# Branch steps dealt out among 64 chunks of a dense layer on ACT and DVE: another table of places, three places in a chunk

## What is computed

```python
x = x + tanh(g_xattn[0]) * wkv(w, u, layernorm(x), ctx)
x = x + tanh(g_ffn[0]) * einsum('bsh,dh->bsd', fwht(silu(xn @ W1.T) * (xn @ W3.T)), W2)   # xn = layernorm(x)
x = x + tanh(g_xattn[1]) * wkv(-exp(time_decay), time_first, layernorm(x), ctx)
x = x + tanh(g_ffn[1]) * moe(layernorm(x))    # top 2 of 8, silu(h1) * h3, combined by gate weights
```

## Time and profile before

| | us |
|---|---|
| three runs | 1480.81, 1480.82, 1476.43 |
| median | 1480.81 |
| the profiled execution | 1483.66 |
| its span | 1482.0 |
| PE, DVE, ACT, POOL busy | 1244.8, 726.9, 504.1, 201.2 |
| the 64 chunks | 113.3 to 743.1 |

### The profile page before, as it was taken

The page is one execution under the profiler, slowest core; times in us unless marked ns, Lnnn a source line. Parts: engine busy times, 40 slices in busy tenths (PEclk is TensorE's granted clock), DMA queues, the critical chain, the costliest instruction groups (busy, mean ns, idle before and its releaser), DMA issues. The chain is left out here.

```text
span 1482.0 us, 18672 instructions
## 1 busy us (share of the span) xinstructions
PE 1244.8 (84%) x5785; PEld 590.9 (40%) x5786; DVE 726.9 (49%) x1175; ACT 504.1 (34%) x671; POOL 201.2 (14%) x206
## 2 busy tenths in 40 slices
...
GB/s 253 29 114 136 178 248 220 171 191 171 254 166 85 181 197 219 214 95 260 213 204 208 46 182 160 146 121 179 186 138 189 178 201 134 163 120 100 77 67 61
DMA packets 228347, 239.13 MB, mean 161 GB/s; under 512 B 137168, under 2 KB 141520, under 8 KB 225168
## 3 DMA queue, kind: packets, MB, share of 16 engines
...
## 5 line engine op out<-in xcount | busy, mean ns | idle before, releaser
L1084 PE MATMUL PS<-weights,xs 128*128 x1872 | 412.9, 381 | 29.5 <-DMA xs<-X 29.5
L1009 PE MATMUL PS<-xs,weights 128*128 128x512 f16 x1536 | 358.4, 390 | 26.8 <-DVE sg L845 15.1
L1084 PEld LDWEIGHTS PS<-weights,xs 128*128 128x128 f16 x1872 | 183.8, 98 | 252.3 <-issue 33.3
L1009 PEld LDWEIGHTS PS<-xs,weights 128*128 128x128 f16 x1536 | 152.6, 100 | 222.9 <-issue 24.2
L912 DVE SCALAR_TENSOR_TENSOR A<-A,PS 128x1024 f32<-128x1024 f32 x39 | 47.6, 1221 | 352.2 <-PE PS L1084 324.1
L1021 PE MATMUL PS<-weights,hs 128*128 128x512 f16 x768 | 181.3, 387 | 0.0
L604 ACT ACTIVATE A<-PS 128x1024 f32<-128x1024 f32 x39 | 39.9, 1024 | 320.1 <-PE PS L1084 192.2
L364 POOL DMA_INDIRECT row_list<-entry,pos x32 | 38.5, 1204 | 790.8 <-DVE pos L795 454.8
L923 DVE TENSOR_SCALAR V<-PS,outl 128x512 f32<-128x512 f32 x39 | 29.3, 751 | 166.7 <-PE PS L1098 150.6
L1021 PEld LDWEIGHTS PS<-weights,hs 128*128 128x128 f16 x768 | 76.4, 100 | 86.2 <-issue 6.6
L1098 PE MATMUL PS<-weights,xs 128*128 x456 | 104.0, 386 | 7.9 <-DMA weights<-e 4.6
...
## 6 DMA issues: line engine op xcount, KB each, us to landing
e<-halves SPq DMA_DIRECT2D x192, 256.0 KB
...
V<-ctx_cm ACTq DMA_DIRECT2D x7, 1024.0 KB, 5.7
X<-w ACTq DMA_DIRECT2D x4, 1024.0 KB, 6.1
out<-X ACTq DMA_DIRECT2D x4, 1024.0 KB, 9.9
...
```

What stands on the lines that cost most here:

```text
L1009: ins = te.matmul(bank(bk), wj[:, j, w, a, c * P:(c + 1) * P], xs[:, g % 2, b, c, :], start=(k == 0 and c == 0), stop=(k == 2 and c == C - 1))
L1084: ins = te.matmul(bank(n), xTt[k][:, b, c, :], weights_of(off, 2 * I // NT * c + n, a), start=(c == 0 and m == 0), stop=(c == C - 1 and m ...
```

## The change

It changes tables and places, no arithmetic.

- UNITS, STEPS, FIRST, GATES, GATE_STEPS and LATE have other numbers. Branches begin 9 or 10 chunks apart. The first branch in the chunks has its own, shorter tail (SHORT). Pieces 2 to 7 are split in chunks 1, 2, 3, 5, 6, 7.
- There are three places. On ACT: place 0 before the silu, place 1 between silu (and first unit) and high copy, place 2 at the chunk's end behind the units. On DVE: place 0 before the product, place 1 behind the low half, place 2 at the end. PE keeps its two.
- k0 takes its own half of the bonus on E1, k1 the other half; den is all scans of V, num has none.
- The turned rows of a post branch go into the place of the group's rows in X (`turned_rows`) and not into E1, except in the last. So xh0 of a post branch waits for the store of those rows (`x3_out`), e0 no longer waits for "last", and the unit buffers in X are lent when "last" of post 0 has run.

```diff
-UNITS = [[3, 3, 3, 3, 0, 3, 3, 3, 2, 3, 3, 3, 4, 4, 4, 2],
-         [3, 3, 3, 2, 4, 4, 4, 4, 2, 3, 4, 3, 2, 3, 3, 3],
...
+UNITS = [[3, 3, 3, 3, 0, 1, 2, 3, 2, 0, 4, 4, 4, 2, 4, 4],
+         [4, 4, 4, 0, 4, 4, 4, 2, 4, 4, 4, 3, 3, 0, 3, 3],
...
-STEPS = [("stats", 0, 0), ("r0", 0, 0), ("newton", 0, 0), ("norm", 1, 0), ("kT0", 1, 1), ("e0", 2, 0), ("k0", 2, 0),
...
+STEPS = [("stats", 0, 0), ("r0", 0, 2), ("newton", 1, 0), ("norm", 1, 1), ("kT0", 2, 0), ("e0", 2, 1), ("k0", 2, 2),
+         ("kT1", 3, 0), ("e1", 3, 1), ("k1", 3, 2), ("ln", 4, 1), ("den", 4, 2), ("rec", 4, 2), ("num", 5, 2), ("mix", 6, 2),
+         ("yT0", 7, 1), ("add0", 8, 0), ("yT1", 8, 1), ("add1", 9, 0), ("r2", 9, 1), ("newton2", 9, 2), ("norm2", 10, 1),
+         ("xT0", 11, 0), ("xh0", 11, 0), ("xl0", 11, 0), ("xT1", 11, 1), ("xh1", 12, 0), ("xl1", 12, 0), ("last", 12, 1),
+         ("raw", 12, 1)]
...
-FIRST = {("pre", 1): 0, ("pre", 2): 11, ("post", 0): 20, ("pre", 3): 30, ("post", 1): 39, ("post", 2): 49}
+FIRST = {("pre", 1): 0, ("pre", 2): 9, ("post", 0): 19, ("pre", 3): 29, ("post", 1): 39, ("post", 2): 49}
...
-GATES = {0: (31, 32, 34, 34, 35), 1: (50, 51, 53, 53, 54), 2: (60, 61, 62, 61, 62)}
+GATES = {0: (38, 41, 44, 44, 45), 1: (54, 58, 58, 59, 59), 2: (62, 63, 63, 63, 63)}
...
-LATE = {1: 2, 2: 3, 4: 4, 7: 5, 9: 6, 10: 7}
+LATE = {1: 2, 2: 3, 3: 4, 5: 5, 6: 6, 7: 7}
...
+        turned_rows = lambda g: E1[:, :] if g == NG - 1 else xg(g)
...
-                            sp.wait_ge(s["x3_out"], 16)
+                            sp.wait_ge(s["side_full"], FILLS.index(("post", 0, "last")) + 1)
...
-                        if posts_before(b):
-                            act.wait_ge(s["side_full"], FILLS.index(("post", posts_before(b) - 1, "last")) + 1)
...
-                        act.activation(ch(E1, a, 2), side, ACT.Copy).then_inc(s["kt_done"], 1)
+                        if g < NG - 1:
+                            act.wait_ge(s["x3_out"], 16 * (g + 1))
+                        act.activation(ch(turned_rows(g), a, 2), side, ACT.Copy).then_inc(s["kt_done"], 1)
...
+                    bonus(layer, E1, SQ, (0, 1))
                 elif step == "k1":
...
-                    bonus(layer, E1, SQ, (0, 1))
+                    bonus(layer, E1, SQ, (2, 3)).then_inc(s["den_done"], 1)
                 elif step == "den":
-                    bonus(layer, E1, SQ, (2, 3)).then_inc(s["den_done"], 1)
-                    scan(layer, A1, V, (0, 1, 2))
+                    scan(layer, A1, V, range(C))
                 elif step == "num":
-                    scan(layer, A1, V, (3,))
```

More of the change, by code:

```diff
@@ L95, in steps_beside @@
         if (kind, gb) in FIRST:
-            found += [(kind, gb, s) for s, d, at in STEPS if FIRST[kind, gb] + d == n and at == place]
+            steps = [(s,) + SHORT.get(s, (d, at)) if (kind, gb) == ("pre", 1) else (s, d, at) for s, d, at in STEPS]
+            found += [(kind, gb, s) for s, d, at in steps if FIRST[kind, gb] + d == n and at == place]
         if kind == "post" and gb in GATES:
@@ L553, in chunk @@
                     w_high(LATE[n])
-                for u in units[0:1]:
-                    unit_high(u)
                 if n >= 2:
```

28 lines of the change are left out of this document (17 added, 11 removed), and 7 rows, old and new, of tables (STEPS, UNITS).

## The result

| | before | after |
|---|---|---|
| median of four runs, us | 1478.62 | 1509.98 |
| lowest to highest | 1476.02 to 1480.82 | 1505.82 to 1513.53 |
| the profiled execution, its span | 1483.66, 1482.0 | 1508.1, 1506.4 |
| the 64 chunks | 113.3 to 743.1 | 111.3 to 773.7 |

The change makes the kernel slower: ratio 1.0212, 95% interval 1.0175 to 1.0249. The forecast was 1486 us with a range up to 1503; the sign was right and the size was not.

A forecast was written before the change was run, and what follows sets the result against it. The 64-chunk loop can't be under 539 us of PE work; 90.7 us were lost. New losses 36.8 + 31.9 + 23.7 + 1.1 + 0.5 + 2.0 = 96.0, 5.3 more: 1486 us, own range 1478 to 1494, with rivals 1456 to 1503.

The forecast's parts named there:

- The waits of kT0 and yT0: PE waits 27.3 us at kT0 opening five chunks, 36.8 with clock; DVE's late mixed rows hold yT0, 4.3 in chunk 26.
- The residual sum in 33: On DVE, the residual sum now behind k1 holds chunk 32's down matmuls by 2.4 us.
- The cost of chunk 63: gate1b, gate2 and ranked stand ahead of DVE's product in chunk 63, and ranked waits for the ranks: 1.1 us.
- norm2: The chain r2, newton2, norm2 gets two chunks, so most of PE's 21.1 us wait for the norm goes.
- The first branch: Early chunks with weight loads: PE waits 17.9 us, plus 3.8 for two clock falls and 2.0 slow start, 23.7 us.
- the price of the clock: Each PE gap of over 2.5 us in the loop was charged 1.9 us of lowered clock.
- clock behind the logits: Logits and ranks of three gates counted as 11 us of the loop's 539 us, with no clock loss behind the logits.
- DVE's part: DVE's chain from k0 to mix makes PE wait 24.3 us; with four clock falls, 7.6 us, it costs 31.9 us.
- The stores: Scatters moved to chunks 45, 59 and 63 meet units' stores there; 2.0 us was taken.
- Rival 3: Two scatters meet four-unit chunks in 45 to 48 and 59 to 61, holding ACT: 15 us more, 1501 us; chance 0.15.
- The new wait for the store of the group's rows: On ACT before xh0 of a second-layer branch, nothing to 3 us each; nothing taken.
- The end and the prologue: Around the loop, steps only move past neighbours on one engine with the same sum: nothing, within 1 us.

The follow-up runs named there:

- a2: Changed kernel with xh1 on ACT ahead of the next branch's norm, xl1 at place 0 of that chunk and newton moved: 1483.5 us, ratio 1.0043.
- d4: The changed kernel run again with no edit: 1514.5 us, ratio 1.0229 to the kernel before.
- c4: The kernel before with the gate's 32 logit matmuls run twice in all four gates, same result: 1507.3 us, ratio 1.0174.
- d2: The changed kernel with its long PE waits filled by 234 extra matmuls where the silu is not late: 1490.1 us, ratio 1.0055.
- a4: The changed kernel with six of the eight units that meet the first scatter moved two chunks later: 1500.8 us, ratio 1.0160.

## Why the prediction failed

**The waits of kT0 and yT0: right.** kT0 4.9, 4.9, 3.3, 8.5, 5.7 forecast in chunks 11, 21, 31, 41, 51; 4.7, 4.7, 4.5, 8.2, 4.3 seen, and a2 shows the cause. yT0 4.3, 4.3, 1.2, 6.8, 5.3 forecast; 4.3, 4.3, 1.1, 6.8, 6.0 seen, with the products' waits. The residual sum in 33 cost 4.0, not 2.4, and 3.4 of clock. The cost of chunk 63 was 1.2 (1.1). norm2 does not wait in chunks 16 to 60, but for 0.3 us.

**The first branch: right in kind, 6 us too high.** 17.6 us, not 23.7. Three loads held ACT as forecast (13.4 us, 3 times), and less of it reached PE: two silu waits of 2.0 and 2.4 in place of 8.8 us in four. In d4 the same kernel lost 19.9 us here, so 2 of the 6 us were luck of the execution. The table load was 1.28 us here too, as in the sum.

**The step that failed: the price of the clock.** The sum charged clock only behind gaps of PE, 1.9 us for each of over 2.5 us, 22.9 us in all with the slow start. 42.7 were lost. That step was wrong in two ways, and the logits are the larger one.

*The clock behind the logits was put at nothing.* They were taken as 3.5 us each in the 539 us of work, with no wait ahead and no clock behind. They lost 11.9 us of clock and 3.0 of idling, in chunks 31, 51 and 61: 14.9 of the 27.4 us. The table brought "last" into the chunk of kT0 and e0; the order showed the wait, but the only row of before that warned of the clock was one fall of 1.7 us behind logits, and it was booked as idling's. c4 shows that the logits do it alone.

*The price per gap was too low for these gaps.* It came from the 31 us that the loop lost beside its idling, over 15 gaps. The clock records have 27.3 us, of which 23.9 behind the 14 waits of over 2 us, 1.7 each, and eleven of these waits were of 2.0 to 3.1 us. It was used for waits of 4 to 8 us, which lose 2.5 to 4.8. d2 shows that this clock is the waits' price. At kT0 and in DVE's part 23.8 us were lost for 17.1 forecast; with the table's means the forecast would be some 10 us higher there (an estimate from the table above).

**The stores: 2.0 forecast, 10.9 seen**, 3.4 of them clock. Rival 3 named the mechanism and its place, and a4 confirms it at the first scatter. At the second it cost PE 0.5 us in the profile of after and 3.1 in d4. The new wait for the store of the group's rows held ACT 0.6 us once and PE never, as forecast.

**The end and the prologue: nothing**, as forecast; the profile of before was a little long there.

Sum against the forecast: logits 14.9, scatter 8.9, kT0 3.3, DVE 4.9, first branch -6.1, and small ones 1.5 make the 27.4 us. That the kernel got slower was forecast with its largest mechanism (kT0: 36.8 us forecast, 40.1 seen); what took it out of the range is mostly clock.
